# A four-layer graph network on one core: every SBUF buffer begins at a multiple of 128 bytes

## What is computed

```python
# layer 0: two graph convolutions, then four passes of an LSTM over windows of p = 1..4 nodes
h = relu(einsum('ts,bsh->bth', adj, x @ Wg0 + bg0))
h = relu(einsum('ts,bsh->bth', adj, h @ Wg1 + bg1))
for p in range(1, MAX_SKIP + 1):
    last = _lstm_last(Wih[p-1], Whh[p-1], bih[p-1], bhh[p-1], windows of p nodes)
    h = h.at[:, idx, :].set(last)            # g = x_t @ Wih.T + h @ Whh.T + bias in each step
# layer 1: attention over 512 edges: leaky_relu(Q[src] + K[dst]), softmax by source node, @ W_out.T
# layer 2: A_hat @ x, @ W1.T (512 wide), batchnorm, relu, @ W2.T, batchnorm
# layer 3: dense attention over the 64 nodes of a graph
Wh = einsum('bnf,fo->bno', h, W); attention = softmax(masked leaky_relu(s1 + s2))
h_prime = einsum('bij,bjo->bio', attention, Wh)
```

## The kernel before

| buffers | before | changed |
|---|---|---|
| `HT`, `H1`, `edge_pairs`, `t_both`, `t_wqv`, `t_wo`, `a_w`, LSTM weights, `b_cell`, `b_gate`, `b_tc` | 0 | 0 |
| LSTM `xs`, `hs` of b = 1 | 0 | 0 |
| LSTM `xs`, `hs` of b = 0; `l_x`, `l_w`, `l_own`, `l_other`, `l_w_hi/lo`, `l_wa`, `l_ident` | 96 | 0 |
| `a_xt`, `a_hT`, `a_xr`, `a_u` | 32 | 0 |
| `c_hT`, `c_keys`, `c_vals`, `c_relu`, `c_attn`, `c_work`, `c_by_dst` | 96 | 0 |
| `w2_hi/lo`, `d_hat`, `d_w1`, `d_xn`, `st1`, `st2` | 32 | 0 |
| `d_h`, `d_ghi`, `d_glo` | 96 | 0 |
| `f_r`, `f_rhi`, `f_rlo` | 0 | 0 |
| `e_y`, `e_xn` / `e_hT`, `e_v`, `e_e`, `e_prob` | 96 / 64 | 0 |
| small columns (`mv`, `ve`, `rstd`, ...) | 0, 32, 64, 96 | 0 |
| slices of `t_sign` used as weights | 8-byte steps | 8-byte steps |

## Time and profile before

### The profile page before, as it was taken

How to read it: one execution, slowest core, us unless ns; L and a number is a source line. 1 busy time by engine, 2 the same in 40 slices (tenths; PEclk the granted TensorE clock), 3 DMA queues, 4 the chain that set the end, 5 groups by cost and what they waited for, 6 DMA issues and landing times. The chain is left out here.

```text
span 2171.2 us, 33706 instructions
## 1 busy us (share of the span) xinstructions
PE 2006.7 (92%) x12342; PEld 1633.7 (75%) x12342; DVE 1272.0 (59%) x2675; ACT 983.2 (45%) x1659; POOL 226.2 (10%) x203
## 2 busy tenths in 40 slices
PE   7998999999999999999996898998988788794998
PEld 6997888888999999888884457575665676574887
DVE  7453665445455555546445665665644677774886
ACT  2544564333333333333323663635443344663785
POOL 1000000000111110110111710101100011200000
PEclk9999999999999999999998999999999899996999
DMA  3201000000100001001013223214140311001232
GB/s 112 78 0 40 0 3 37 0 0 0 39 1 0 0 0 29 1 1 78 0 62 113 70 77 110 96 43 136 50 148 1 98 58 39 12 8 41 78 106 79
DMA packets 83053, 100.05 MB, mean 46 GB/s; under 512 B 8976, under 2 KB 75152, under 8 KB 80656
## 3 DMA queue, kind: packets, MB, share of 16 engines
q1 hardware_dynamic: 82960, 98.79, 13.8%
HBM read 61.78 MB, written 33.55 MB: 44 GB/s over the span
## 5 line engine op out<-in xcount | busy, mean ns | idle before, releaser
L669 ACT ACTIVATE b_gate<-b_pG,b_bias 128x512 f32<-128x512 f32 (+1 forms) x504 | 304.0, 632 | 369.6 <-PE b_pG L54 368.6
L52 PE MATMUL b_pG<-b_xshi,b_whi 128*128 128x512 f32 (+1 forms) x1008 | 370.0, 367 | 6.4 <-DVE b_xslo L726 5.8
L54 PE MATMUL b_pG<-b_xshi,b_wlo 128*128 128x512 f32 (+1 forms) x1008 | 370.5, 368 | 0.0
L53 PE MATMUL b_pG<-b_xslo,b_whi 128*128 128x512 f32 (+1 forms) x1008 | 370.2, 367 | 0.0
L722 DVE CAST b_xshi<-HT 128x512 fp32r<-128x512 f32 (+3 forms) x144 | 59.7, 456 | 275.7 <-PE b_pG L54 275.5
L52 PEld LDWEIGHTS b_pG<-b_xshi,b_whi 128*128 128x128 f32 x1008 | 190.1, 189 | 36.0 <-DVE b_xslo L726 6.0
L53 PEld LDWEIGHTS b_pG<-b_xslo,b_whi 128*128 128x128 f32 x1008 | 189.9, 188 | 28.6
L54 PEld LDWEIGHTS b_pG<-b_xshi,b_wlo 128*128 128x128 f32 x1008 | 190.0, 188 | 27.6
L54 PE MATMUL b_pG<-b_hshi,b_wlo 128*128 128x512 f32 (+1 forms) x576 | 207.2, 360 | 0.0
L53 PE MATMUL b_pG<-b_hslo,b_whi 128*128 128x512 f32 (+1 forms) x576 | 206.4, 358 | 0.0
L52 PE MATMUL b_pG<-b_hshi,b_whi 128*128 128x512 f32 (+1 forms) x576 | 206.1, 358 | 0.0
(11 more groups left out here) (341 smaller groups left out, 3981.3 us busy)
## 6 DMA issues: line engine op xcount, KB each, us to landing
a_xt<-in_x SPq DMA_DIRECT2D x16, 512.0 KB, 5.8
h_scratch<-HT SPq DMA_DIRECT2D x4, 2048.0 KB, 7.6
l_x<-in_x SPq DMA_DIRECT2D x16, 512.0 KB, 4.0
l_w<-h_scratch SPq DMA_DIRECT2D x16, 512.0 KB, 5.1
x_scratch<-l_x SPq DMA_DIRECT2D x16, 512.0 KB, 3.1
c_x<-x_scratch SPq DMA_DIRECT2D x32, 256.0 KB, 3.7
x_scratch<-c_x SPq DMA_DIRECT2D x32, 256.0 KB, 2.4
l_x<-x_scratch SPq DMA_DIRECT2D x16, 512.0 KB, 3.8
```

Source lines behind the costliest of these rows:

```text
L52: nc.tensor.matmul(out, w_hi, x_hi, start=first, stop=False)
L53: nc.tensor.matmul(out, w_hi, x_lo, start=False, stop=False)
L54: return nc.tensor.matmul(out, w_lo, x_hi, start=False, stop=last)
L669: nc.scalar.activation(gate[s][:, g, 0:plan.n], pG[s][:, g, 0:plan.n], SIG[g], bias=bias[:, plan.p - 1, 2 * g + s:2 * g + s + 1])\
```

## The change

Three edits. `allocator` fills the gap to the next multiple of 128 before every buffer. `Placed` steps in multiples of 128 unless told otherwise, and the fixed offsets of `Late` become multiples of 128 (212960 to 212864, 212448 to 212352, 208352 to 208256). In `Tables` the tables grow from 21600 to 21888 bytes; the scratch buffers of the table building keep steps of 32, and `s_an` moves from one scratch area to the other to make room.

```diff
+LINE = 128
 def allocator(nc, ctx):
     def sb(name, shape, dt=F32):
+        at = -(-nc.sbuf_base // 32) * 32
+        gap = -at % LINE // 4
+        if gap:
+            ctx.enter_context(nc.sbuf_tensor(name + "_gap", [P, gap], F32))
         return ctx.enter_context(nc.sbuf_tensor(name, shape, dt))
 class Placed:
-    def __init__(self, nc, at):
-        self.nc, self.at = nc, at
+    def __init__(self, nc, at, unit=LINE):
+        self.nc, self.at, self.unit = nc, at, unit
...
-        self.at += -(-4 * words // 32) * 32
+        self.at += -(-4 * words // self.unit) * self.unit
 class Late:
-    ROWS_AT, CONSTS_AT, RANK_AT = 212960, 212448, 208352
+    ROWS_AT, CONSTS_AT, RANK_AT = 212864, 212352, 208256
 class Tables:
-    BYTES = 21600
+    BYTES = 21888
...
-        sb = Placed(core.nc, at + self.BYTES)
+        sb = Placed(core.nc, at + self.BYTES, 32)
...
-        self.eye2, self.adj2, self.an_t2, self.scaled = (sb("s_" + n, [P, NODES]) for n in ("eye2", "adj2", "an_t2", "scaled"))
+        self.eye2, self.adj2, self.an_t2, self.an, self.scaled = (
+            sb("s_" + n, [P, NODES]) for n in ("eye2", "adj2", "an_t2", "an", "scaled"))
...
-        sb = Placed(core.nc, at + self.BYTES + 4 * NODES * NODES)
+        sb = Placed(core.nc, at + self.BYTES + 4 * NODES * NODES, 32)
...
-        self.an, self.diag = sb("s_an", [P, NODES]), sb("s_diag", [P, NODES])
+        self.diag = sb("s_diag", [P, NODES])
```

## The result

The changed kernel takes 2158.49 us (median of 4 runs, 2155.62 to 2159.25) beside 2173.36 for the kernel before (4 runs): a ratio of 0.9941, 95% interval 0.9928 to 0.9953. The medians differ by 14.9 us here and by 12.2 there. The forecast was 2157.5. The total came out as forecast, and the largest term within 0.9 us; the reason given for it did not hold, and two smaller terms rested on that reason and failed.

What follows compares the result with a forecast made beforehand. The prediction took TensorE's matmul pitch, gapless in the LSTM, as the bound. Savings of 10.2 (LSTM), 1.3 (GCN), 2.0 (edge attention), 1.3 (`f_`) and 0.3 (dense attention) summed to 15.1 us, giving 2157.5 us; range 2147 to 2165.

Steps and rivals of the forecast that it cites:

- The bound and the size: LSTM stage: TensorE streams matmuls without a gap; 1464 of 512 columns save 6.4 ns each, -10.2 us with b = 1 entries.
- Either operand off 128 bytes seems to cost some 6 ns: All 512-column matmuls: one operand off a multiple of 128 bytes costs some 6 ns, both no more than one.
- The GCN, -1.3 us: GCN stage: 224 products of 512 columns go from 232.8 to 227.1 ns, -1.3 us.
- The 256-column products, 0: GCN's second product, attention outputs and dense attention: 256-column products taken as unchanged; 4.1 ns gain each kept for the range.
- `f_`, -1.3 us: Second convolution product: 384 matmuls save 4.9 ns, 1.9 us, half passed on in 8 of 16 groups; -1.3 us (0 to 2.5).
- A: Rival, chance 0.18: only the moving operand's alignment matters, so just LSTM and GCN gain, 11.5 us, giving 2161.1 us.
- The edge attention, -2.0 us: Edge attention: 980 matmuls of 512 columns save 2.7 ns in short runs, part absorbed by waits; -2.0 us (0 to 5.3).
- `d_`, 0: First convolution product: TensorE waits for a VectorE and ScalarE loop, so savings only lengthen its wait; 0 (at most 2.4 us).
- The other engines, 0: VectorE, ScalarE and GpSimd: durations do not depend on the addresses, so columns with lines of their own give 0.
- B: Rival, chance 0.09: the b = 0 buffers' place at the top of SBUF matters, not the multiple; no change, 2172.6 us.
- C: Rival, chance 0.04: operands beginning alike collide, costing 13 ns for each of 1844 matmuls outside the LSTM; slower, 2185 us.
- D: Rival, chance 0.07: 256-column products gain too and other stages pass all on; 20.9 us saved, 2151.7 us.

Runs made afterwards that it cites:

- the first experiment: Kernel before with only the fixed place of the long-lived row buffers moved from 212960 to 212864: 2159.76 us, ratio 0.9945.
- the first kernel of the last pair: Kernel before with the rows' constants 160 bytes lower and a 56-word pad ahead of the b = 1 rows, giving LSTM distances 192 and 224: 2183.21 us.

## Why the prediction was right, and where it was not

**The bound and the size: right.** The start-to-start distance of matmuls in the gapless LSTM was the right view, 1464 matmuls the right count, and 6.4 ns nearly the right price (6.8 measured, since both b settle at 226.67 once no slow stream goes ahead). The term was -10.2 us and measured -11.1: -9.8 for b = 0 against 9.4, -0.65 for b = 1 against 0.9, and -0.65 in pass 3, which I had put at nothing from the earlier trace rows, though its step-1 units were dearer.

**"Either operand off 128 bytes seems to cost some 6 ns": wrong.** The earlier trace rows had one pair of distances, 96 and 0, and I read them as one operand off 128 and none off. The rest, three streams near 233 ns in other stages, suited both readings, since all of them had a distance other than 0. What would have shown it: offsets written modulo 256 and 512 too, not only modulo the number in the change. The rearrangement 128 bytes lower refutes the step, the one at 224 modulo 256 shows what stands in its place.

**The GCN, -1.3 us: failed.** Its distance went from 32 to 128, and its pitch from 232.8 to 231.1. That is worth 224 x 1.7 = 0.4 us, and the dearer 256-column products take 448 x 1.6 = 0.7 us back. The stage moved by -0.3 us in one profile and +0.2 in the other. At distance 0 the pitch was 227.4.

**The 256-column products, 0: off the other way.** My two bounds were 0 and a gain of 4.1 ns; in the kernel after they cost 1.6 ns more, at distance 128, and 2.4 more with all at distance 0, (256 + 32) / 2.4 GHz. The range had no room below zero, though nothing in the rows excluded it.

**`f_`, -1.3 us: failed.** The pitch in the run shown stayed 233.5 ns, the time of the stage 101.98 to 102.86 us against 101.89. The test that I had named, "227 to 229 ns parts the forecast from A", pointed to A, and A was wrong as well: moving aligned data, `f_` was slow before and after. With the pitch at 227.7 its stage was 100.8 to 102.1 us; at equal time at half clock that is about 1 us less, near what the half-passed-on guess said of a faster stream.

**The edge attention, -2.0 us: no gain shows.** Its distance went from 160 to 128, its pitch fell by about 1 ns, so 980 products can have given 1 us. The -4.5 us of one profile is +0.5 in the other. The kernel with the rows 128 bytes lower, where all else is as in the kernel after, had an LSTM of 957.58 us (-1.8) and a time 1.6 us under the one before: nothing is left for the rest. All twelve traces say the same. As an estimate, take from each `c_` stage half of its time at half clock: six kernels with the places of before give 523.5 to 525.7 us, four with those of the kernel after 524.5 to 526.4.

**The dense attention, -0.3 us: too small to see.** Whatever the places, its stage takes 189.3 to 189.8 us in the traces with 29 us at half clock and 191.8 to 192.8 in those with 35.

**`d_`, 0: right.** Here the distance did become 0 and the pitch of the full runs fell from 233.3 to 227.5 ns, and the stage went from 145.12 to 144.79 us. The rows that answer to the earlier trace rows:

```profile
1754.21 2.05 PE L1750 MATMUL d_pA<-d_hat,d_h 128*128 128x128 f32 x16 [0.94 <-ACT d_h L1781]
...
1763.26 2.05 PE L1750 MATMUL d_pA<-d_hat,d_h 128*128 128x128 f32 x16 [0.96 <-ACT d_h L1781]
```

The group still takes 9.05 us, and TensorE's wait for `d_h` grew from 0.82 to 0.94 us: what a stream saves there goes into the wait.

**The other engines, 0: right**. Of their groups of over 3 us in all, one moved by more than 1% on average, VectorE's `l_w` from 1189 to 1165 ns (0.8 us in 32 instructions); it takes 1146 to 1191 over the twelve traces and doesn't go by the layout.

**The rivals.** A's total, 2161.1, lies near the measurement, but its mechanism is refuted by the rows 128 bytes lower. B (no change, it is the place) fell with the first experiment; of the two rules of the Trainium skill that stood beside it, neither agrees: the address alone moves a 512-column matmul from 226.7 to 234.2 ns, where its page "TensorE: Matmul & The Clock Gate", section "Wait — 56ns, not 53.3ns?", has a fixed 2.5 ns over the columns, 215.7. C, equal phases collide, has the sign reversed at 512 columns. It has a grain of truth at 256. D, more than forecast, had the 256-column products faster; they became dearer.

The sum of 15.1 us against 12.2 to 14.9 measured was thus right by one good term and by luck in the others: 4.9 us of it were put down to stages that gave 0 to 2, and the LSTM gave 0.9 more.

## What to carry to other kernels

Where TensorE streams float32r matmuls of 512 columns without a gap, read the distance from start to start and compare it with (columns + 32) / 2.4 GHz; if it is 6 ns longer, give the moving operand and the weights the same offset modulo 256 bytes. Aligning each to 128 leaves the distance at 0 or at 128, as it happens, and 128 costs as much as an unaligned one. Of a regularity in one pair of rows write down every reading that the addresses allow, and test one that parts them before a whole layout is changed. And where a stage has half-clock pieces, run one program twice before putting a few us of it down to an edit.

## What the runs showed of the hardware

The pitch of a 512-column float32r matmul with new weights each time depends on the distance of its operands modulo 256 bytes, from 226.7 to 234.2 ns, and not on their own offsets (distance 0 at 128 on 128 and at 224 on 224, distance 64 at 192 on 128 and at 32 on 224). At distance 0 it is the columns plus 32 cycles of 2.4 GHz at 512 (226.67), 336 (153.33) and 256 columns (120.0). At 256 columns other distances are cheaper: 117.6 ns at 224. At 336 columns the step-2 units show 153.3 ns at distance 0 and at 96, but 156.0 at 192, in all four of them (the first kernel of the last pair). The time at half clock differs between executions of one program, and a stage's length with it, by 5 us in `c_` and 3 us in `e_`, while the LSTM stage took 947.9 to 948.5 us in seven runs with distance 0.
